# Opening of a fused attention and expert layer: first keys' loads on ScalarE's queue, value buffers for six pairs, the sixth pair earlier, ones in pieces

## The reference

```
a   = causal attention of LN(x), 16 heads of 16, then the output projection
x1  = x + LN(a)
h   = LN(x1)
p   = softmax(h @ router^T + bias);  the two best of 8 experts, p not renormalised
y   = sum over both: p_e * (W_down_e . act(W_gate_up_e h) + bias)
out = x1 + LN(y)
```

## Time and profile before

| | us |
|---|---|
| median of 3 runs | 2096.94 |
| lowest and highest | 2094.99, 2099.21 |
| the profiled execution: its own time | 2098.84 |
| its span in the profile | 2097.1 |
| TensorE busy of the span | 1961.6 (94%) |
| VectorE, ScalarE, GpSimd busy | 1589.2, 1337.7, 949.0 |

### The profile page before, as it was taken

One profiled execution on the slowest core, in us unless ns is written; L12 is line 12 of the kernel. 1 busy time (PEld: TensorE's weight loads), 2 busy tenths in 40 slices (PEclk: granted clock), 3 DMA queues, 4 the chain that ended last, 5 costly groups with the idle time before them and its releaser, 6 DMA issues. The chain is left out here.

```text
span 2097.1 us, 50455 instructions
## 1 busy us (share of the span) xinstructions
PE 1961.6 (94%) x13630; PEld 1303.1 (62%) x13631; DVE 1589.2 (76%) x5427; ACT 1337.7 (64%) x3413; POOL 949.0 (45%) x1442
## 2 busy tenths in 40 slices
PE   6799999999999999999999999999999999999970
PEld 4344444444444444444433338999999999999970
DVE  2877788888888888888888837778777777777757
ACT  3377777777777777777777685455454545454436
POOL 5233344455655646556455553555333333333327
PEclk9799999999999999999999999999999999999995
DMA  7633546465454544545445458888999989898868
GB/s 205 190 112 121 178 146 206 141 191 175 148 175 134 182 148 150 178 133 173 135 152 178 136 191 245 245 237 257 260 266 258 268 255 266 257 267 232 241 181 320
DMA packets 259745, 416.09 MB, mean 198 GB/s; under 512 B 37088, under 2 KB 195296, under 8 KB 252384
## 3 DMA queue, kind: packets, MB, share of 16 engines
q1 hardware_dynamic: 219936, 369.37, 54.7%
q0 software_dynamic: 29824, 35.54, 9.5%
q10 hardware_dynamic: 9792, 8.93, 1.4%
HBM read 290.74 MB, written 122.41 MB: 197 GB/s over the span
## 5 line engine op out<-in xcount | busy, mean ns | idle before, releaser
L1014 ACT ACTIVATE arena<-ps_e 128x512 f32<-128x512 f32 (+3 forms) x1536 | 687.3, 493 | 276.4 <-PE ps_e L1234 266.2
L649 DVE CUSTOM_DVE_ANT_0 arena<-ps_s,c 128x128 bf16<-128x128 f32 (+3 forms) x1024 | 479.1, 481 | 60.7 <-PE ps_s L1215 56.8
L1215 PE MATMUL ps_s<-arena 96*128 96x512 bf16 (+3 forms) x1536 | 489.3, 333 | 25.4 <-DMA arena<-qk_parts 7.0
L1234 PE MATMUL ps_e<-arena 98*128 98x512 bf16 (+3 forms) x1536 | 483.3, 329 | 2.9 <-ACT arena L1014 2.3
L652 DVE TENSOR_REDUCE cmax<-ps_s 128x1 f32<-128x512 f32 x512 | 351.2, 686 | 142.2 <-PE ps_s L1215 138.7
L1215 PEld LDWEIGHTS ps_s<-arena 96*128 96x128 bf16 x1536 | 152.1, 101 | 356.6 <-DVE cmax L649 90.8
L1253 PE MATMUL ps_o<-arena 128*32 128x512 f32 (+3 forms) x3072 | 329.9, 502 | 4.9 <-ACT ot L1028 3.5
L546 POOL TENSOR_SCALAR_AFFINE_SELECT arena<-arena 128x512 f32<-128x512 f32 x256 | 162.4, 635 | 295.3 <-ACT arena L1014 294.9
L530 POOL DMA_INDIRECT acc<-blank,place_now x136 | 217.5, 1599 | 137.7 <-DMA acc<-blank,place_now 71.1
L1369 PE MATMUL ps_s<-arena 128*128 128x128 f32 x2192 | 269.5, 276 | 0.0
L1369 PEld LDWEIGHTS ps_s<-arena 128*128 128x128 f32 x2192 | 263.4, 193 | 5.5 <-ACT arena L1156 0.6
(11 more groups left out here) (183 smaller groups left out, 3058.3 us busy)
## 6 DMA issues: line engine op xcount, KB each, us to landing
arena<-in_gate_up SPq DMA_DIRECT2D x92, 1024.0 KB, 6.2
arena<-qk_parts SPq DMA_DIRECT2D x384, 128.0 KB, 2.9
c_h<-in_gate_up SPq DMA_DIRECT2D x48, 1024.0 KB, 6.0
qk_parts<-space SPq DMA_DIRECT2D x120, 192.0 KB
d_xin<-xs SPq DMA_DIRECT2D x141, 130.5 KB, 2.9
v_aug<-space SPq DMA_DIRECT2D x32, 512.0 KB, 4.9
arena<-v_aug SPq DMA_DIRECT2D x32, 512.0 KB, 5.0
o_t<-ot SPq DMA_DIRECT2D x64, 256.0 KB, 2.8
```

The lines of the kernel that those rows point to most:

```text
L649: dve.tensor_tensor_reduce(summed[:, m % RJ, 0:w], ps_s[:, m % RS, 0:w], after[:, HALF - w:HALF], 1.0, LOWEST, ALU.add, ALU.max, dst).then ...
L1014: act.activation(pw[:, n % RP, 0:w], ps_e[:, n % RE, 0:w], ACT.Exp, scale=SCALE).then_inc(e_done, 1)
L1215: pe.matmul(ps_s[:, m % RS, 0:w], qs[0:ROWS, slot, i * P:(i + 1) * P], ks[0:ROWS, slot, k0:k0 + w], start=True, stop=True).then_inc(s_scor ...
L1234: pe.matmul(ps_e[:, n % RE, 0:w], ks[0:ROWS_M, slot, j * P:(j + 1) * P], qs[0:ROWS_M, slot, q0:q0 + w], start=True, stop=True).then_inc(e_ ...
```

## The change

It touches the opening only:

- The pairs 0 to 5 are moved four slots forward in A_AT and V_AT: A_AT begins with -40, -37, -34, -31, -27, -20 and V_AT with -26, -25, -24, -23, -21, -14. The entries from pair 6 on stay. SLOTS begins four slots earlier.
- Pairs 2 to 5 get value buffers of their own (`vout_of`): pairs 2 and 3 in the space of the value sets of quads 1 and 2, pairs 4 and 5 in four places of the exponentials' ring. VectorE sets these to one as well. ScalarE's copies of pairs 2 to 5 wait for no store; in slot -1 it waits once for the value stores of pairs 4 and 5.
- The six loads of quad 0's keys are issued by ScalarE in slot -21, the six of its queries by SyncE in slot -18. In `load_rows` the order of all loads is first queries, then keys.
- SyncE stores the parts and values of pair 4 in slot -17, after what it does in slot -18 (before: slot -16); those of pair 5 in slot -13 (before: -9). It issues x of pairs 6 and 7 in slot -16.
- GpSimd's memset of the keys' rows 96 and 97 is three memsets, one for each set, in slots -20, -12 and -9.

```diff
--- before.py
+++ after.py
@@ -81,8 +81,8 @@
     HEAD_SLOTS = NM // 4
     BEGIN = -AHEAD * HEAD_SLOTS
     EARLY = 4
-    A_AT = [BEGIN - 18 + 3 * a for a in range(EARLY)] + [BEGIN - 5, BEGIN + 2] + [NE * (a - 6) - 4 for a in range(6, PAIRS)]
-    V_AT = [BEGIN - 4 + a for a in range(EARLY)] + [start + 6 for start in A_AT[EARLY:]]
+    A_AT = [BEGIN - 22 + 3 * a for a in range(EARLY)] + [BEGIN - 9, BEGIN - 2] + [NE * (a - 6) - 4 for a in range(6, PAIRS)]
+    V_AT = [BEGIN - 8 + a for a in range(EARLY)] + [start + 6 for start in A_AT[EARLY:]]
     FIRST_EVEN = 6
     LATE = PAIRS - PER
     C_AT = [NE * (r + 4) + 3 for r in range(LATE)] + [NE * QUADS + d for d in (3, 8, 26, 30)]
@@ -291,6 +291,15 @@
         def xn_t_of(a):
             return pw[:, 12 + a].rearrange("p (k t) -> p k t", k=KT) if a < EARLY else xn_t[:, a % 2]
 
+        def vout_of(a):
+            if 2 <= a < EARLY:
+                at = 13312 + (a - 2) * 1024
+            elif EARLY <= a < EARLY + 2:
+                at = 16384 + (6, 10)[a - EARLY] * HALF
+            else:
+                return vout[:, a % 2]
+            return arena[:, at:at + 1024].rearrange("p (s c h d) -> p s c h d", s=4, c=2, h=4)
+
         def parts_of(a):
             if 2 <= a < EARLY:
                 three = pw[:, 3 * (a - 2):3 * (a - 1)].rearrange("p a b -> p (a b)")
@@ -317,21 +326,20 @@
             row = engine.value_load(zero_at[0:1, e:e + 1], min_val=0, max_val=E * REGION - P)
             engine.dma_start(xs[bass.ds(row, P), :], nobody[:]).then_inc(zeros_out, 16)
 
+        def load_rows(engine, quad, w):
+
+            b, s, u = quad // 4, quad % 4, quad % SETS
+            for nth, part in enumerate(((0, 0, 0, 1, 1, 2), (0, 1, 2, 0, 1, 0))[w]):
+                engine.dma_start((qs, ks)[w][nth:ROWS:ROWS // DH, u * 4:u * 4 + 4].rearrange("r h t -> r (h t)"),
+                                 qk_v[b, w, s // 2, s % 2, part]).then_inc(loads[u], 16)
+
         block = ctx.enter_context(nc.Block())
 
         @block.sync
         def _(sp):
             def load_heads(quad):
-
-                b, s, u, nth = quad // 4, quad % 4, quad % SETS, 0
-                for z, often in ((0, 3), (1, 2), (2, 1)):
-                    for k in range(often):
-                        rows = slice(nth, ROWS, ROWS // DH)
-                        sp.dma_start(qs[rows, u * 4:u * 4 + 4].rearrange("r h t -> r (h t)"),
-                                     qk_v[b, 0, s // 2, s % 2, z]).then_inc(loads[u], 16)
-                        sp.dma_start(ks[rows, u * 4:u * 4 + 4].rearrange("r h t -> r (h t)"),
-                                     qk_v[b, 1, s // 2, s % 2, k]).then_inc(loads[u], 16)
-                        nth += 1
+                load_rows(sp, quad, 0)
+                load_rows(sp, quad, 1)
 
             def load_values(quad):
                 sp.dma_start(vs[:, quad % SETS], v_aug[quad // 4, quad % 4]).then_inc(v_loads[quad % SETS], 16)
@@ -340,7 +348,7 @@
                 u, b, j = a % 2, a // PER, a % PER
                 sp.wait_ge(a_vout, a + 1)
                 sp.dma_start(v_aug[b, :, :, 2 * j:2 * j + 2].rearrange("s p c h d -> p s (c h d)"),
-                             vout[:, u].rearrange("p s c h d -> p s (c h d)")).then_inc(v_out[u], 16)
+                             vout_of(a).rearrange("p s c h d -> p s (c h d)")).then_inc(v_out[u], 16)
 
             def slots(j):
                 return sp.value_load(table[0:1, 0, bass.ds(j, 1)], min_val=0, max_val=DUMMY + (SPARE - 1) * P)
@@ -379,7 +387,7 @@
                     load(n + RX, n % RX)
                     sp.wait_ge(gu_ps, 2 * n + 2)
                     load_weights(n + WX, n % WX, later=(n + WX >= BESIDE))
-                for a in pairs_due(7, 9, g):
+                for a in due([max(start + (7 if a < FIRST_EVEN else 9), BEGIN + 1 if a >= EARLY else SLOTS.start) for a, start in enumerate(A_AT)], 0, g):
                     u, b, j = a % 2, a // PER, a % PER
                     sp.wait_ge(a_p3, 2 * a + 2)
                     for m in range(4):
@@ -387,7 +395,7 @@
                                      parts_of(a)[:, :, m]).then_inc(qk_out[u], 16)
                     if a >= EARLY:
                         store_values(a)
-                for a in pairs_due(-1, -9, g):
+                for a in due([BEGIN + 2 if a in (4, 5) else start - (1 if a < FIRST_EVEN else 9) for a, start in enumerate(A_AT)], 0, g):
                     if EARLY <= a + 2 < PAIRS:
 
                         sp.wait_ge(a_xn, a - 1 if a < EARLY else a + 1)
@@ -395,7 +403,7 @@
                 if g == BEGIN:
                     for u in range(2):
                         sp.wait_ge(qk_out[u], EARLY // 2 * Q_STORES * 16)
-                    load_heads(0)
+                    load_rows(sp, 0, 0)
                     for a in range(EARLY):
                         store_values(a)
                     for early in range(1, SETS):
@@ -534,10 +542,11 @@
                 return pool.value_load(table[0:1, 2, bass.ds(n, 1)], min_val=16, max_val=TILES // 2 * 16)
 
             for g in SLOTS:
-                if g == BEGIN:
-                    pool.wait_ge(a_p3, 2 * EARLY + 1)
-                    pool.memset(ks[ROWS:ROWS_M], -1.0).then_inc(ones, 1)
-                    pool.wait_ge(ones, 1)
+                for u, (at, done_by, n) in enumerate(((BEGIN - 2, a_p3, 2 * EARLY + 2), (BEGIN + 6, a_p3, 2 * EARLY + 4), (BEGIN + 9, s_mlo, 2))):
+                    if g == at:
+                        pool.wait_ge(done_by, n)
+                        pool.memset(ks[ROWS:ROWS_M, u * 4:u * 4 + 4], -1.0).then_inc(ones, 1)
+                        pool.wait_ge(ones, u + 1)
                 if 0 <= g < NE * QUADS and g % NE in DIAGONAL:
                     quad, c = divmod(g, NE)
                     at = c * 4 % RP
@@ -625,7 +634,10 @@
 
         @block.vector
         def _(dve):
-            dve.memset(vout, 1.0).then_inc(v_ones, 1)
+            dve.memset(vout, 1.0)
+            for a in range(EARLY, EARLY + 2):
+                dve.memset(vout_of(a), 1.0)
+            dve.memset(arena[:, 13312:15360], 1.0).then_inc(v_ones, 1)
             for sel in sels.values():
                 dve.memset(sel[:], 0.0).then_inc(sel_set, 1)
             for e in range(E):
@@ -1072,6 +1084,13 @@
 
             for g in SLOTS:
                 quad, c = divmod(g, NE)
+                if g == BEGIN - 3:
+                    for u in range(2):
+                        act.wait_ge(qk_out[u], EARLY // 2 * Q_STORES * 16)
+                    load_rows(act, 0, 1)
+                if g == -1:
+                    for u in range(2):
+                        act.wait_ge(v_out[u], (EARLY + 2) // 2 * 16)
                 for s in range(4):
                     if 0 <= g + 1 < NE * QUADS:
                         exponential(g + 1, s)
@@ -1101,11 +1120,11 @@
                         for a in due(V_AT, 0, g):
                             u = a % 2
                             act.wait_ge(a_v, a + 1)
-                            if a >= 2:
+                            if a >= EARLY + 2:
                                 act.wait_ge(v_out[u], a // 2 * 16)
                             bank = ps_e[:, 1 + a % 2] if a < EARLY else ps_w[:]
                             for t in range(2):
-                                last = act.activation(vout[:, u, :, t, :, 0:DH],
+                                last = act.activation(vout_of(a)[:, :, t, :, 0:DH],
                                                       bank[:, t * D:(t + 1) * D].rearrange("p (s h d) -> p s h d", s=4, h=4), ACT.Copy)
                             last.then_inc(a_vout, 1)
                         for a in pairs_due(-2, -10, g):
@@ -1390,7 +1409,7 @@
                 if g == BEGIN:
                     pe.wait_ge(a_r1, 2 * EARLY)
                 if g == -1:
-                    pe.wait_ge(ones, 1)
+                    pe.wait_ge(ones, SETS)
                     pe.wait_ge(a_vout, EARLY)
                 for s in range(4):
                     m = (g - BEGIN) * 4 + s
```

## The result

| | us |
|---|---|
| before, median of 4 runs | 2098.07 (2094.99 to 2100.42) |
| after, median of 4 runs | 2129.39 (2126.80 to 2131.07) |
| ratio | 1.0144, 95% interval 1.0132 to 1.0156 |
| profiled execution after: time, span | 2131.07, 2129.4 |

The change makes the kernel 31.3 us slower. The forecast was 22.7 us slower, 2119.6 us, with a range up to 2127.0 us; the measured median is 2.4 us above that range.

What follows compares the result with a forecast made beforehand. TensorE's pace bounds the kernel once exponentials run, so opening delays reach the end. First maximum +22.9 us, 18 slots -0.2 us: +22.7 us on the median 2096.94 us gives 2119.6 us, range 2112 to 2127 us.

Steps and rivals of the forecast that it cites:

- The deciding step: Opening: SyncE issues pair 6's x after VectorE wants it in slot -20; first maximum at 78.5 us against 55.59, +22.9 us.
- The 18 slots: Window from first maximum to first exponentials' scores, 43.35 us before: +1.4 first head, -1.6 second and third, sum -0.2 us.
- rival C: Clock: TensorE idles some 20 us, second head takes 9.0 us for 6.9; +2.1 us, 2121.7 us; chance 0.08.
- SyncE's path: Opening: seven steps of SyncE's issues from its start to pair 6's x landing at 77.6 us.
- steps 3 and 4: SyncE: four value stores of pairs 0 to 3, 1.9 us; 24 loads of quads 1 and 2, 15.9 us, to 65.8 us.
- 1 start: SyncE's start: 42.6 us plus 1.6 us left from VectorE's new memsets, so 44.2 us.
- 2 six loads: SyncE: six of quad 0's twelve loads stay, 0.636 us each, 3.8 us, to 48.0 us.
- 7 to VectorE's start: Pair 6's x issued at 71.1 us behind a backlog lands 6.5 us later, at 77.6 us; then VectorE's statistics.
- Rival A: SyncE's and ScalarE's issues exclude each other: +3.8 us on SyncE's path, 2123.4 us; chance 0.12.
- Rivals B: Pair 6's x lands 2.6 us after issue, not 6.5: -3.9 us, with the window's -2 about 2114 us; chance 0.10.
- D: Not slower: pair 6's x is there at slot -20, first maximum about 55.3 us, 2093 to 2097 us; chance 0.05.
- Keys on ScalarE's queue: Opening: ScalarE's six key loads land at 54.8 us, no gain for first scores; cost on SyncE's path taken as 0.

Runs made afterwards that it cites:

- plain delay: Kernel before with 15 more memsets of the value buffers at the head of VectorE's program, each waiting for the one before: 2131.26 us, ratio 1.0158.

## Why the prediction was wrong in size and right in kind

**The deciding step was right.** Pair 6's x is issued after VectorE asks for it; undoing that one slot takes back 19 of 26.65 us in the attention, and doing it alone costs 23.7 us. The signs named ahead are there: the wait at the statistics (34.26 us), TensorE idle for 20.67 us, no store wait on ScalarE, the later stretches unchanged up to 1130 us. The 18 slots took 43.91 us against 43.15 forecast, though not head by head: 8.6, 9.2 and 6.6 us for the first three, and 9.0, 6.9 and 7.9 before. I had +1.4 us for the first, and it was -0.4; I had -1.6 for the next two, and it was +0.9. The second head has the 9.2 us that rival C feared, at a granted clock of 0.77, but it isn't the long idle time that makes it: it took 9.2 us as well where the first head ran at 1.00. VectorE waits 2.3 us for scores in it, with matmuls of pair 5 in between, and had no wait in the second head of before.

**Where the miss lies.** The measured median is 9.8 us above the forecast: 3.8 us of it lie in the opening, 4.8 us after it, and 1.1 us are the median of before, which came out higher with a fourth run. With the opening's part alone the time would have been 2123.4 us, inside my range. So two terms failed: the opening's, which the runs explain, and the stretches behind it, which I had at no cost and whose extra stays open.

**The terms of SyncE's path that failed are steps 3 and 4.** I had x issued at 71.1 us and it was issued at 74.50.

| step | forecast us | measured us |
|---|---|---|
| 1 start | 44.2 | 42.97 |
| 2 six loads | 3.8 | 3.84 |
| 3 four value stores | 1.9 | 4.16 |
| 4 24 loads | 15.9 | 17.86 |
| 5 value loads | 1.5 | 1.49 |
| 6 pair 4's stores | 3.8 | 4.18 |
| 7 to VectorE's start | 6.5 | 6.11 |

(each measured one from the start of a line to the start of the next). Steps 3 and 4 cost 4.2 us more than forecast; the start, which I had 1.2 us too late, hides a part of it. I priced these steps by issue times from an execution in which the four stores were held apart by ScalarE's copies. I subtracted that wait of 4.1 us as pure loss, but in it the DMA engines had worked off a part of the 2 MB of stores. Without it the stores come back to back, and the issues behind them slow down. The value buffers alone, in the kernel before, show it too: 3.6 us for the four stores and 17.1 for the 24 loads, with nothing on ScalarE's queue. The first two of these loads take more than twice the usual time:

```profile
53.92 1.34 SPq L339 DMA_DIRECT2D arena<-qk_parts  x1
55.30 1.35 SPq L341 DMA_DIRECT2D arena<-qk_parts  x1
56.70 0.60 SPq L339 DMA_DIRECT2D arena<-qk_parts  x1
```

Where ScalarE's wait is still there (before, and before with x of pair 6 late) the 24 loads took 15.9 and 15.8 us. Stores and loads together took 20.7 to 21.2 us in the four kernels with these buffers and nothing on ScalarE's queue, and 21.6 to 22.0 in four executions with the keys there and the stores ahead. So about 3 of the 4.2 us are the stores, and about 1 us is the keys on ScalarE's queue, for which I had taken 0.

**Rival A gave the opening's number by the wrong mechanism.** It asked for +3.8 us on SyncE's path. The opening was indeed late by 3.8 us more than I had it (26.53 for 22.7), but only 3.0 of them lie on that path (the statistics at 80.61 us for 77.6) and 0.8 in the window, and the path's are mostly the stores'. That the sum fits is luck. And in the run with the value stores moved back each issue keeps its length of about 0.6 us with both queues busy, so they don't exclude each other. The Trainium skill (Perfetto Trace Analysis, "DMA Instruction — HWDGE (DVE, Sync)") has the one generator locked for exclusive use until the descriptors of a DMA are generated, and says that the issue shown in a profile holds the wait for the lock and more besides. I had read the whole 0.6 us as locked; by these rows it isn't, and how much of an issue is, no run here shows. Rivals B and D fell: x took 6.1 us from its issue to VectorE's start, not 2.6, and the wait was there.

**The memsets and the start.** The cast came at 7.51 us, 2.3 us late where I had 1.6: each memset has a small gap ahead. SyncE began only 0.4 us late all the same. Part of that is that one load of x was gone ahead of it, and with the memsets by GpSimd it began between 41.48 and 42.82 us in seven runs, so executions differ here by more than what is left to explain.

**Keys on ScalarE's queue.** I had them begin at 48.4 and end at 52.2 us; they began at 46.56 and ended at 53.79, with scores at 58.79 for my 54.8. That they bring the first scores nothing was right, and it is worse than nothing: the first maximum came at 57.25 us with them and at 51.73 us with all twelve on SyncE's queue. It stayed hidden under VectorE's wait.

**After 1130 us.** The range took 1.5 us for the median. The medians of the one changed kernel against before were +31.3 and +27.8 us, with the opening the same to 0.3 us. Over all runs the end differs from the attention's shift by -1.3 to +4.7 us, with a plain delay at +0.2 and pair 6's x alone at -0.3. So I take most of it as spread of the late stretches, which my range should have held: its upper end was +30 us against the median that I forecast from. One of the steps is shown not to be the change's. From the output store that stands at 1198.50 us in the profile of before to the one at 1211.63 it takes 13.1 us there, 14.6 and 14.9 us in the two profiles of the changed kernel, but also 15.0 us in the kernel before with x of pair 6 late and 14.9 us in the one with value buffers and x of pair 7 early. The step near the 36th expert tile is an idle time of TensorE of 2.41 us at 1523 us for which the profile shows no cause. Between attention and end, the nine sets of runs of kernels built on the change average +1.6 us and the four sets of kernels built on before +0.5, so a real cost of about 1 us behind the opening isn't excluded. What makes the spread stays open.

## What to carry to other kernels

When a load is moved to a later slot, look for its consumer on every engine by slot number, not only for the data hazard: a semaphore that was always met is not in the profile, and it becomes the wait that holds everything. A wait on an issuing queue is also time in which the DMA engines work off what was issued; when it is removed, price the transfers behind it by bytes as well as by issues. And when a fix makes an opening faster, look at the next load of the same kind, which had just been hidden.

## What the hardware showed

- SyncE's and ScalarE's hardware queues issue side by side: medians of 590 and 611 ns with both busy, and SyncE's were 0.59 us with its queue alone. What they share is the DMA engines (a share of 0.57 with one queue of such loads, 0.99 with two): the loads then landed after 5.1 us in the median instead of 2.6. The Trainium skill (DMA: Bandwidth & Descriptors, "Issuing engines are not separate DMA queues") says that all run on the same 16 engines and only issue time is saved; this agrees.
- Behind 2 MB of value stores the issues themselves get longer: 1128 ns in the median on ScalarE's queue, where they were 611 ns without the stores. A high share of the DMA engines alone doesn't do it: it was 1.02 from 46.2 to 52 us in the one run and 0.99 in the other. ScalarE's compute instructions stand behind them, 5.79 us here.
- The first head, with the same VectorE work, took 10.6 us at a granted clock of 0.57 and 7.2 us at 1.00. Ahead of the one TensorE had idled 6.1 us in one piece, behind the value copy that stood behind ScalarE's key loads; ahead of the other no idle time was over 1.4 us. The length of one idle time doesn't order the runs, though: after 6.1 us with the memsets by GpSimd the first head took 8.3 us at 0.81, and after 3.1 us with the value stores moved back it took 10.6 us at 0.56. What sets the clock here stays open.
- Not every head gets longer with the clock: the fourth head, which has no matmuls of a pair in it, took 7.2 us at a granted clock of 0.50 in the changed kernel and 7.2 us at 0.71 in the kernel before.
